# Last layer's attention: row maxima taken per bank of 512 columns, the second unit of a step issued behind the values, the reciprocal in four pieces, the maxima turned one step earlier

## The reference, cut to what matters

```
x  = group_norm(x)                                    # 32 groups
q, k, v = split(x @ W_qkv + b_qkv)                    # 8 heads of 64
for each image and head:
    s   = q @ k.T * 64**-0.5                          # 1024 x 1024
    p   = softmax(s)                                  # over the keys
    o   = p @ v                                       # 1024 x 64
out = x_in + concat(o) @ W_out + b_out
```

## Time and profile before

| | us |
|---|---|
| median of 3 runs | 4650.07 |
| profiled execution | 4645.78 |
| its span | 4644.0 |
| first matmul of the attention's first pass (pair 0) | at 4070.77 |
| step 0 of pair 0 | at 4110.34 |
| step 0 of pair 7 | at 4538.32 |
| first matmul of the output projection | at 4583.17 |

### The profile page before, as it was taken

One profiled execution on the slowest core, in us unless ns is written; L12 is line 12 of the kernel. 1 busy time (PEld: TensorE's weight loads), 2 busy tenths in 40 slices (PEclk: granted clock), 3 DMA queues, 4 the chain that ended last, 5 costly groups with the idle time before them and its releaser, 6 DMA issues. The chain is left out here.

```text
span 4644.0 us, 65947 instructions
## 1 busy us (share of the span) xinstructions
PE 4177.0 (90%) x19516; PEld 2352.9 (51%) x19516; DVE 2894.8 (62%) x4078; ACT 2530.4 (54%) x4526; POOL 990.1 (21%) x684
## 2 busy tenths in 40 slices
PE   2599999999999999999989997769989977878988
PEld 1355555555555555555567775234444443344443
DVE  7877777777777777777773333556766533244442
ACT  3588888888888888888864332111221210112221
POOL 1401111011111111011105445022222100035553
PEclk7799999999999999999999998889999978989999
DMA  1200000000000000000020000387666412442211
GB/s 42 84 2 2 2 2 2 2 2 2 2 2 2 2 2 2 2 2 2 2 74 1 0 0 14 125 332 261 235 214 232 168 43 79 155 100 50 61 37 73
DMA packets 97301, 280.43 MB, mean 60 GB/s; under 512 B 33120, under 2 KB 34144, under 8 KB 78016
## 3 DMA queue, kind: packets, MB, share of 16 engines
q0 software_dynamic: 20736, 151.00, 9.2%
q1 hardware_dynamic: 76480, 128.39, 9.1%
HBM read 224.38 MB, written 54.85 MB: 60 GB/s over the span
## 5 line engine op out<-in xcount | busy, mean ns | idle before, releaser
L572 DVE SCALAR_TENSOR_TENSOR cpb_r<-cpb_z,cpb_r 128x512 fp32r<-128x512 f32 x2052 | 1321.8, 686 | 491.8 <-ACT cpb_r L547 486.0
L547 ACT ACTIVATE cpb_r<-cpb_z 128x512 fp32r<-128x512 f32 x2052 | 1121.2, 605 | 277.7 <-PE cpb_z L479 277.7
L553 ACT ACTIVATE cpb_h<-cpb_z,net_vec 128x512 f32<-128x512 f32 x1536 | 1020.5, 714 | 2.0 <-PE cpb_z L495 2.0
L492 PE MATMUL cpb_z<-cpb_r,cpb_w2a 128*128 128x512 f32 x2048 | 856.7, 418 | 3.0
L493 PE MATMUL cpb_z<-cpb_r,cpb_w2b 128*128 128x512 f32 x2048 | 803.5, 392 | 0.0
L495 PE MATMUL cpb_z<-cpb_r,cpb_w2a 128*128 128x512 f32 x2048 | 797.3, 389 | 0.0
L430 POOL TENSOR_TENSOR cpb_exp<-l0k_posx,l0k_pos 128x1024 bf16 (+1 forms) x130 | 247.4, 1903 | 1966.1 <-PE cpb_z L479 1947.0
L1322 PE MATMUL dc_pc<-dc_sc,l_dcw 128*128 128x512 f32 x1152 | 533.7, 608 | 6.5 <-ACT dc_dc L1377 6.5
L492 PEld LDWEIGHTS cpb_z<-cpb_r,cpb_w2a 128*128 128x128 f32 x2048 | 384.1, 188 | 189.8 <-issue 123.3
L504 PE MATMUL cpb_zo<-cpb_h,cpb_w3w 128*32 128x512 f32 x3584 | 477.3, 605 | 0.0
L495 PEld LDWEIGHTS cpb_z<-cpb_r,cpb_w2a 128*128 128x128 f32 x2048 | 385.3, 188 | 85.2
(11 more groups left out here) (318 smaller groups left out, 4542.2 us busy)
## 6 DMA issues: line engine op xcount, KB each, us to landing
corners<-cf_tt SPq DMA_DIRECT2D x77, 256.0 KB, 3.6
qk_parts<-gn_r SPq DMA_DIRECT2D x64, 256.0 KB, 2.0
l_dcw<-in_dc_wT SPq DMA_DIRECT2D x9, 1024.0 KB, 10.9
bias_dram<-cpb_bst SPq DMA_DIRECT2D x520, 8.0 KB
net_x<-in_x SPq DMA_DIRECT2D x8, 1024.0 KB, 8.8
sa_qa<-qk_parts SPq DMA_DIRECT2D x16, 512.0 KB, 9.2
sa_ka<-qk_parts SPq DMA_DIRECT2D x16, 512.0 KB, 11.2
l_w<-in_mlp_w1T SPq DMA_DIRECT2D x1, 4096.0 KB, 23.7
```

The costliest lines, as they stand in the source:

```text
L492: pe.matmul(z2[:, bank, :], W2A[:], R1[:, k, :], start=True, stop=False)
L547: act.activation(R1[:, t % RING, :], z1[:, t % 4, :], ACT.Relu).then_inc(r1_ready, 1)
L553: act.activation(H2[:, t % 8, :], z2[:, t % 3, :], ACT.Relu, bias=V("cpb_b2")).then_inc(h2a, 1)
L572: v.scalar_tensor_tensor(R2[:, t % RING, :], z1[:, t % 4, :], 0.0, R1[:, t % RING, :].bitcast(F32), ALU.max, ALU.subtract).then_inc(r2_rea ...
```

## The change

```diff
+        MXP = s.sb("mxp", [P, UNITS, 2])
-        AT_STEP = [0, 1, 2, 2, 3, 4, 5, 6, 6, 7, 8, 9, 10, 11, 12, 13]
-        TURN = 14
+        AT_STEP = [0, 1, 2, 2, 3, 4, 5, 6, 6, 7, 8, 9, 9, 10, 11, 12]
+        TURN = 13
+        SUMS_1, SUMS_0 = 3, 10
+        PIECES = 4
+        PW = NF // PIECES
-        def row_bank_uses(pair, n):
+        def maxima_taken(pair, n, half):
             if pair == 0:
                 return max(0, n - 1)
-            return pair * UNITS + n
+            return max(UNITS, UNITS + ((pair - 1) * UNITS + n) * 2 - 1 + half)
...
# SP: load(pair)
+                if pair >= SLOTS:
+                    sp.dma_start(QB[DH:DH + 2, j].bitcast(F32), ZERO[:].unsqueeze(1).broadcast_to([2, 2, HW])
+                                 ).then_inc(loaded[j], 16)
...
# GpSimd, ahead of its loop
+            for j in range(SLOTS):
+                pool.memset(KB[DH:DH + 2, j]..., -1.0).then_inc(rows_set, 1)
+                pool.memset(QB[DH:DH + 2, j]..., 0.0).then_inc(zeroed, 1)
+            pool.wait_ge(rows_set, SLOTS)
+            pool.wait_ge(zeroed, SLOTS)
+            pool.memset(ZERO[:], 0.0).then_inc(zeroed, 1)
...
# PE: first_pass
-                if row_bank_uses(pair, n):
-                    pe.wait_ge(max_done, row_bank_uses(pair, n))
                 for half in range(2):
+                    if maxima_taken(pair, n, half):
+                        pe.wait_ge(max_done, maxima_taken(pair, n, half))
                     pe.matmul(out[:, half, :], QA..., KA..., start=True, stop=False)
-                    mm = pe.matmul(out[:, half, :], QB..., KB..., start=False, stop=True)
-                mm.then_inc(a_mm, 1)
+                    pe.matmul(out[:, half, :], QB..., KB..., start=False, stop=True).then_inc(a_mm, 1)
...
# PE: a step
                     for u in range(2):
                         second_pass(pair, u, c)
+                    units = [n for n in range(UNITS) if AT_STEP[n] == c]
                     if pair + 1 < GS:
-                        for n in range(UNITS):
-                            if AT_STEP[n] == c:
-                                first_pass(pair + 1, n)
+                        if units:
+                            first_pass(pair + 1, units[0])
                         if c == TURN:
                             turn_maxima(pair + 1)
                     values(...)                        # of the step before, as it was
-                    if c == 3 and pair:
+                    if c == SUMS_1 and pair:
                         sums(pair - 1, 1)
-                    if c == 11:
+                    if c == SUMS_0:
                         sums(pair, 0)
+                    if pair + 1 < GS and len(units) > 1:
+                        first_pass(pair + 1, units[1])
...
# DVE
             def unit_max(pair, n):
+                if pair == 0: one reduction of 1024 columns, as it was
+                else:
+                    for half in range(2):
+                        v.wait_ge(a_mm, (pair * UNITS + n) * 2 + half + 1)
+                        v.tensor_reduce(MXP[:, n, half:half + 1], pa[:, half, :], AX.X, ALU.max).then_inc(max_done, 1)
             def maxima(pair):
                 if pair:
+                    v.wait_ge(max_done, UNITS + pair * UNITS * 2)
+                    v.tensor_tensor(MX[:], MXP[:, :, 0], MXP[:, :, 1], ALU.max).then_inc(m_joined, 1)
...
-                v.reciprocal(RC[:], psm[:]).then_inc(rec_done, 1)
+                v.reciprocal(RC[:, cols], psm[:, cols]).then_inc(rec_done, 1)     # invert(): one of four pieces of 128 columns
...
-                    v.wait_ge(b_mm, pair * 2 * STEPS)
-                    v.memset(QB[DH:DH + 2, (pair + 2) % SLOTS]..., 0.0).then_inc(zeroed, 1)
...
-                    if c == 3 and pair:
-                        divide(pair - 1, 1)
-                    if c == 11:
-                        divide(pair, 0)
+                    for half, first in ((1, SUMS_1), (0, SUMS_0)):
+                        h = pair * 2 + half - 2 * half
+                        if h >= 0 and first <= c < first + PIECES:
+                            invert(pair - half, half, c - first)
+                        if h >= 0 and c == first + PIECES - 1:
+                            scale(pair - half, half)
```

More of the change, by code:

```diff
@@ L1795, in layer3_attention @@
         RC = s.sb("rc", [P, NF])
-        ONE, NEG = s.sb("one", [P, DH]), s.sb("neg", [P, 1])
+        ONE, ZERO = s.sb("one", [P, DH]), s.sb("zero", [2, HW])
+        MXP = s.sb("mxp", [P, UNITS, 2])
         pa, pb = s.ps("pa", [P, 2, NF]), s.ps("pb", [P, 2, NF])
@@ L1799, in layer3_attention @@
         pt, psm = s.ps("pt", [2 * UNITS, NF]), s.ps("psm", [P, NF])
-        ones_set, neg_set, rows_set, zeroed = s.sem("ones_set"), s.sem("neg_set"), s.sem("rows_set"), s.sem("zeroed")
+        ones_set, rows_set, zeroed = s.sem("ones_set"), s.sem("rows_set"), s.sem("zeroed")
         a_mm, max_done, m_step, m_mm, mt_done = (s.sem(n) for n in ("a_mm", "max_done", "m_step", "m_mm", "mt_done"))
+        m_joined = s.sem("m_joined")
         b_mm, exp_done, pv_mm, added, sum_mm, rec_done, out_ready = (
@@ L1808, in layer3_attention, with loads @@
         block = s.block()
-        AT_STEP = [0, 1, 2, 2, 3, 4, 5, 6, 6, 7, 8, 9, 10, 11, 12, 13]
-        TURN = 14
+        AT_STEP = [0, 1, 2, 2, 3, 4, 5, 6, 6, 7, 8, 9, 9, 10, 11, 12]
[3 more added lines that the diff above has]
+        PW = NF // PIECES
         def bank(pair, n):
             return (pa, pb)[n % 2] if pair == 0 else pa
-        def row_bank_uses(pair, n):
+        def maxima_taken(pair, n, half):
             if pair == 0:
                 return max(0, n - 1)
-            return pair * UNITS + n
+            return max(UNITS, UNITS + ((pair - 1) * UNITS + n) * 2 - 1 + half)
+        def loads(pair):
+            return sum(6 if p < SLOTS else 7 for p in range(pair % SLOTS, pair + 1, SLOTS))
         @block.sync
@@ L1856, in _ @@
             load(2)
+            sp.wait_ge(zeroed, SLOTS + 1)
             sp.dma_start(g["W_OUT"][:], d["w_out"].rearrange("(k p) m -> p k m", p=P)).then_inc(wo_in, 16)
@@ L1871, in _ @@
         def _(pool):
+            for j in range(SLOTS):
+                pool.memset(KB[DH:DH + 2, j].rearrange("p u n -> p (u n)").bitcast(F32), -1.0).then_inc(rows_set, 1)
+                pool.memset(QB[DH:DH + 2, j].rearrange("p u n -> p (u n)").bitcast(F32), 0.0).then_inc(zeroed, 1)
+            pool.wait_ge(rows_set, SLOTS)
+            pool.wait_ge(zeroed, SLOTS)
+            pool.memset(ZERO[:], 0.0).then_inc(zeroed, 1)
+            pool.wait_ge(zeroed, SLOTS + 1)
             pool.memset(ONE[:], 1.0).then_inc(ones_set, 1)
@@ L1892, in first_pass @@
                 j, cols, out = pair % SLOTS, slice(c * P, (c + 1) * P), bank(pair, n)
-                if row_bank_uses(pair, n):
-                    pe.wait_ge(max_done, row_bank_uses(pair, n))
                 for half in range(2):
+                    if maxima_taken(pair, n, half):
+                        pe.wait_ge(max_done, maxima_taken(pair, n, half))
                     keys = slice(half * NF, (half + 1) * NF)
                     pe.matmul(out[:, half, :], QA[:, j, u, cols], KA[:, j, u, keys], start=True, stop=False)
-                    mm = pe.matmul(out[:, half, :], QB[:, j, u, cols], KB[:, j, u, keys], start=False, stop=True)
-                mm.then_inc(a_mm, 1)
+                    pe.matmul(out[:, half, :], QB[:, j, u, cols], KB[:, j, u, keys], start=False, stop=True
+                              ).then_inc(a_mm, 1)
             def turn_maxima(pair):
@@ L1930, in sums @@
                 if h:
-                    pe.wait_ge(rec_done, h)
+                    pe.wait_ge(rec_done, h * PIECES)
                 for u in range(2):
@@ L1938, in _ @@
             pe.wait_ge(zeroed, SLOTS)
-            pe.wait_ge(loaded[0], 96)
+            pe.wait_ge(loaded[0], loads(0) * 16)
             for n in range(UNITS):
@@ L1946, in _ @@
                         if pair + 1 < GS:
-                            pe.wait_ge(loaded[(pair + 1) % SLOTS], ((pair + 1) // SLOTS + 1) * 96)
-                            pe.wait_ge(zeroed, SLOTS + max(0, pair + 2 - SLOTS))
+                            pe.wait_ge(loaded[(pair + 1) % SLOTS], loads(pair + 1) * 16)
                         pe.wait_ge(values_in[pair % 2], (pair // 2 + 1) * 32)
@@ L1993, in unit_max @@
             def unit_max(pair, n):
-                v.wait_ge(a_mm, pair * UNITS + n + 1)
-                v.tensor_reduce(MX[:, n:n + 1], bank(pair, n)[:].rearrange("p h n -> p (h n)"), AX.X, ALU.max
-                                ).then_inc(max_done, 1)
+                if pair == 0:
+                    v.wait_ge(a_mm, n * 2 + 2)
+                    v.tensor_reduce(MX[:, n:n + 1], bank(0, n)[:].rearrange("p h n -> p (h n)"), AX.X, ALU.max
+                                    ).then_inc(max_done, 1)
+                else:
+                    for half in range(2):
```

(38 more changed lines are left out.)

## The result

The changed kernel takes 4575.85 us, median of four runs (4571.09 to 4580.41), the kernel before 4645.38 beside it (4639.52 to 4652.29): ratio 0.985, 95% interval 0.9829 to 0.987. The difference of the medians is 69.5 us. The profiled execution has a span of 4578.6 us, 65.4 less than the one before (4644.0). Timed once more with five runs on another occasion it took 4576.49, ratio 0.9845 (0.9832 to 0.9859).

The account below looks back on a forecast made before the run. PE was taken as the bound, itself waiting for DVE's maxima (33.2 us) and the maxima rows' DMA (26.1). Saved 69.6, less 4.2 and 0.5, gave 64.9: 4580.9 or 4585.2 by baseline, so 4583 us; range 4571 to 4607.

Parts of the forecast that it names:

- L: Last attention, step 0 of pair 0 to step 0 of pair 7: from 427.98 us to near 363.
- Part 1: Two-unit steps: second unit behind the values, maxima per bank; halves 0.69 us, no wait, steps at 4.02.
- Part 2: DVE's reciprocal in four pieces of 0.95 us each; the 1.38 over at steps 5 and 13 goes.
- Part 3: Maxima turned at step 13: the 1.77 us wait for their rows is covered with 0.37 to spare.
- the turning: Turning at step 13 comes late, its join waiting for POOL's additions: 0.6 us a pair, 4.2 over seven.
- the low clock behind it has no cause: Step 0 of each pair: with the 1.77 us wait covered, the 1.54 us of low clock goes too.
- Part 4: Zero rows to a seventh DMA, -1 rows and first zeros to POOL: seven memsets, 11.7 us, at no price.
- the 0.5 charged for them: Very end of the attention: four reciprocal pieces in a row cost 3.8 us in place of 3.36, +0.5.
- The rule of the Trainium skill: A two-SBUF-input VectorE instruction and a GpSimd instruction reading SBUF contend, the later waiting out the other: 4.2 us, without it 0.

Follow-up runs that it names:

- the halves alone: Changed kernel with old unit table, turning at step 14 and whole reciprocals at steps 3 and 11, keeping maxima per bank and second unit behind the values: 4602.8 us.
- the turning undone: Changed kernel with the old table of units and the maxima turned at step 14 (also called the turning at 14): one run 4583.6 us.
- the pieces alone: Kernel before plus the moved -1 and zero rows and the reciprocal in four pieces, whole reductions, turning at step 14: one run 4625.8 us.
- the rows alone: Kernel before with only the -1 and zero rows moved (GpSimd memsets ahead, a seventh DMA in a load): one run 4648.8 us.
- the join experiment: Changed kernel with the two halves' maxima joined by a reduction with one SBUF input, not an elementwise maximum of two: one run 4576.6 us.
- the turning alone: Kernel before plus the moved -1 and zero rows, the changed table of units and the maxima turned at step 13: one run 4669.6 us.

## Why the prediction was right, point by point

The forecast was 4583, measured 4575.85; as a difference, 64.9 forecast and 69.5 measured between the medians, 65.4 between the profiled executions. In these L fell by 67.3, while pair 0's first pass began 2.6 later than before (4073.36 and 4070.77), behind layers that the change doesn't touch.

- **The stretch L.** Forecast 363 (358.4 and 4.2 for the turning), measured 360.65. L holds the gain: from step 0 of pair 7 to the first matmul of the projection 44.85 before and 44.80 after.
- **Part 1**, right by mechanism and size: halves of 686 ns, steps of two units at 4.10 against 4.02 expected, of which 0.1 comes back in the step behind (2.96 and 3.83 where 3.08 and 3.93 stood). Shown by undoing each edit: 19.8 and 14.4 us.
- **Part 2**, right: pieces of 937 ns; steps 5 and 12, which ask for the unit that DVE would reduce behind a whole reciprocal, take 3.07 and 3.06, and 4.07 or 4.08 with the reciprocal whole again.
- **Part 3**, right in its three claims (the wait for the rows goes, the turning is late next, the join waits for POOL's addition), and too dear in one term: I charged 0.6 a pair for the turning, step 13 shows 2.63 - 2.25 = 0.38, 2.7 us in all and not 4.2. I had let the join take its 0.2 after POOL's additions; it ended 0.03 behind them. One row that the price rested on was read loosely: the first layer's 0.69 "beside an idle POOL" (2446.63 to 2447.32) ran 0.25 into POOL's first addition (from 2447.07), having begun ahead of it. Wrong is what it says of the clock: "the low clock behind it has no cause", meaning the wait of 1.77 as the cause. The halves alone and the turning undone both keep that wait (1.70 and 1.3) and have no fall; the pieces alone have it in one of six pairs, the rows alone in four. So 9.2 us of the sum (1.54 in six pairs) were booked to this part, which by its undoing is worth 8.4 to 9.3 in all and not the 21 of the waits (11.7) and the low clock (9.2) together. That the sum came out even so is luck in this term: all of the falls went, by whichever edit.
- **Part 4**, right: POOL's six memsets of 2048 columns took 1.80 us each over two partitions, the seventh, of 1024, took 0.94, and all were done at 4066.5; the first matmul came at 4073.36, and L didn't move with the rows alone. The last four pieces took 3.39 and not 3.8, less than four times 0.937; so the 0.5 charged for them didn't come:

```profile
4513.69 3.39 DVE L2045 RECIPROCAL sa_rc<-sa_psm 128x128 f32<-128x128 f32 x4 [10.76 <-PE sa_psm L1953]
```

- **The rule of the Trainium skill** (SBUF — State Buffer, "Who interferes with whom"): the join's 0.97, ending with POOL's addition, against 0.19 for the form with one input beside the same additions, agrees with it. The same section lists `cast` among the instructions that can contend; the cast's 0.75 in the join experiment, against 0.18 beside an idle POOL, agrees too; the expectation had gone by two inputs alone and so named the wrong instruction.
- **The parts don't add.** Alone they gave -45.1 (halves and order), -17.8 (pieces) and +27.1 (turning), together -35.8; all three gave -67.3. (Counted from 429.95, the kernel with the rows alone, they are -47.1, -19.8 and +25.2, together -41.7, against -69.3.) The change also has the sums a step earlier, which none of the three alone has. The terms of the prediction were taken with the others in place, and undoing them shows what each is worth there.
- In the rows ahead of the prediction, the label of group 6 says pair 3's maxima; those at 4226.85 are pair 2's, as the prediction's text has them.

What stays open is what makes the clock fall. Shown is: no fall in any pair from 1 to 6 where PE's only waits are 0.2 to 0.6 us and one of up to 1.9 in a pair (the halves alone, and the turning at 14); falls at varying places where waits of 1.1 to 1.3 us stand at two to four places in a pair (the kernel before, the rows alone, the pieces alone, the turning alone), and behind each of the seven waits of 2.8 in the last. No kernel here changed the distance between waits alone.

## What to carry to other kernels

A wait that an engine pays for another can be worth more than it shows: here 43.5 us of waits took 17 us of low clock with them, and 7 that their brackets don't count. Before work is asked for earlier, look whether its producer stands behind something long on its own engine, and clear that first: the earlier turning lost 27 us alone and gained 8 to 9 beside the other edits. And of two forms of a small DVE instruction beside GpSimd's additions, take the one with one input from SBUF, and see what follows it.

## What the runs showed of the hardware that was not expected

- A wait of 1.70 us of PE in a stretch with the clock at 1.00 left it there, six times of six; the same wait in the kernel before had 1.5 us of low clock behind it in all six pairs, where another wait of 1.1 us stood some 8 us ahead. That other wait alone doesn't decide it either: with the rows alone both stood there, and two of six pairs had no fall.
- A DVE instruction of 16 columns takes 0.18 us beside an idle POOL and up to 1.18 beside its additions of 128x512; the join (0.97), the cast (0.43 to 0.75) and the subtraction (1.18) were each seen to do so. In the turning alone the cast ended at 4292.64, 0.04 behind the first of two additions that stand back to back (4291.34 and 1.26 long), and the subtraction 0.03 behind the second.
- Pair 0's maxima rows, four DMAs of 4 KB, reached PE 15.8 us after the turning behind about 4 MB of loads issued ahead of them, and 4.7 us after it once the loads were issued behind them.
